# Window attention block: value products ahead of the denominators, sums in a scores' bank, another order of POOL's image bias, values in 64-wide tiles

## What is computed

```
y  = ln(x) rolled by (-4, -4), cut into windows of 64 tokens
q, k, v = y @ qkv_w.T + qkv_b          # q scaled by 16 ** -0.5
p  = softmax(q @ k.T + mask)           # mask: -100 across the seam of the roll
x  = x + unroll(p @ v @ proj_w.T + proj_b)
x  = x + gelu(ln(x) @ mlp_w1.T + mlp_b1) @ mlp_w2.T + mlp_b2
out = x * rsqrt(einsum('nchw,ic->nihw', x * x, gamma) + beta)
```

## Time and profile before

| what | value |
|---|---|
| median of three runs | 1836.98 us |
| the profiled execution | 1833.88 us, span 1832.1 us |
| granted TensorE clock | 0.996 |
| busy: PE, DVE, ACT, POOL | 93%, 81%, 82%, 20% of the span |
| instructions | 83,025 |

### The profile page before, as it was taken

How to read it: one execution, slowest core, us unless ns; L and a number is a source line. 1 busy time by engine, 2 the same in 40 slices (tenths; PEclk the granted TensorE clock), 3 DMA queues, 4 the chain that set the end, 5 groups by cost and what they waited for, 6 DMA issues and landing times.

```text
span 1832.1 us, 83025 instructions
## 1 busy us (share of the span) xinstructions
PE 1712.4 (93%) x33524; PEld 1446.9 (79%) x33524; DVE 1483.5 (81%) x4142; ACT 1501.8 (82%) x2957; POOL 358.5 (20%) x459
## 2 busy tenths in 40 slices
PE   6899999999999999999999999999999999999995
PEld 4788888888888888788888888888888788788784
DVE  5888888888888888888888888888888888888872
ACT  2788888888888888888888888888888888888885
POOL 1112122122121221211221221221221221221211
PEclk9999999999999999999999999999999999999998
DMA  2111221121121121121121122122122122112111
GB/s 55 51 52 54 57 59 54 55 61 55 52 63 54 51 64 55 51 65 53 51 66 53 51 63 56 51 63 56 52 61 57 52 59 59 52 55 63 41 36 33
DMA packets 179168, 100.37 MB, mean 55 GB/s; under 512 B 26868, under 2 KB 178790, under 8 KB 178790
## 3 DMA queue, kind: packets, MB, share of 16 engines
q1 hardware_dynamic: 178228, 94.96, 18.6%
q10 hardware_dynamic: 562, 0.11, 0.0%
HBM read 32.05 MB, written 25.17 MB: 31 GB/s over the span
## 4 chain that ended last, share of the span: by engine, by line
PE 62%; DVE 19%; ACT 11%; issue 6%; DMA 1%; SPq 0%; POOL 0%; DVEq 0%; ACTq 0%; POOLq 0%
PE mm_bank L1107 9%; PE mm_bank L904 8%; PE score_banks L934 6%; PE mm_bank L902 5%; PE mm_bank L1104 5%; PE mm_bank L1092 5%; DVE mean_gap L732 5%; DVE stats L719 5%; PE pv_bank L1057 4%; ACT y_hi L542 4%; ACT y L536 4%; DVE v_block L781 4%; PE turn_banks L940 3%; DVE y_lo L768 3%; PE mm_bank L1071 3%
## 5 line engine op out<-in xcount | busy, mean ns | idle before, releaser
L512 ACT ACT_TABLE_LOAD x256 | 328.4, 1283 | 4.6
L591 ACT ACTIVATE hidden<-mm_bank 128x512 f32<-128x512 f32 x384 | 232.3, 605 | 85.7 <-PE mm_bank L1092 73.7
L1104 PE MATMUL mm_bank<-hidden,w 128*32 128x384 f32 x2304 | 275.0, 490 | 7.0 <-ACT log_sum L577 0.3
L1107 PE MATMUL mm_bank<-hidden,w 128*32 128x128 f32 x2304 | 275.7, 274 | 0.0
L562 ACT ACTIVATE probs<-shifted 128x384 f32<-128x384 f32 x512 | 249.3, 520 | 27.3 <-DVE shifted L797 24.5
L467 POOL TENSOR_TENSOR x<-x,b_bias 128x384 f32<-128x384 f32 x128 | 105.9, 827 | 836.8 <-PE turn_banks L926 836.8
L768 DVE TENSOR_TENSOR y_lo<-turn_banks,y_hi 96x512 fp32r<-96x512 f32 x128 | 87.9, 687 | 194.4 <-ACT y L536 191.4
L1107 PEld LDWEIGHTS mm_bank<-hidden,w 128*32 128x32 f32 x2304 | 242.9, 110 | 0.5
L573 ACT ACTIVATE probs_t<-score_banks 128x512 f32<-128x512 f32 x384 | 219.2, 613 | 0.0
L790 DVE TENSOR_REDUCE row_max<-score_banks 128x6 f32<-128x384 f32 x384 | 209.5, 546 | 0.0
L797 DVE TENSOR_TENSOR shifted<-score_banks,row_max 128x384 f32<-128x384 f32 x384 | 198.8, 544 | 0.0
(11 more groups left out here) (110 smaller groups left out, 4616.1 us busy)
## 6 DMA issues: line engine op xcount, KB each, us to landing
x_ext<-in_x SPq DMA_DIRECT2D x128, 192.0 KB, 3.1
k_block<-k SPq DMA_DIRECT2D x256, 96.0 KB, 2.0
out<-o_ext SPq DMA_DIRECT2D x64, 192.0 KB, 2.4
x_ext<-in_x SPq DMA_DIRECT2D x128, 48.0 KB, 2.8
attended<-attended SPq DMA_DIRECT2D x384, 16.0 KB, 1.8
x<-x SPq DMA_DIRECT2D x384, 16.0 KB, 1.8
out<-o_ext SPq DMA_DIRECT2D x64, 96.0 KB, 2.0
out<-o_ext SPq DMA_DIRECT2D x128, 48.0 KB, 2.2
```

The source lines that it names most:

```text
L512: nc.scalar.preload_act_table_set(name)
L591: nc.scalar.activation(hidden[:, n, :], mm_bank(f"mlp1_{n}", A)[:, :], ACT.Gelu)\
L1104: nc.tensor.matmul(to[group(j), 0:MAIN], w2[:, n, group(j)], hidden[:, n, 128:HALF], start=first, stop=last)
L1107: made = nc.tensor.matmul(to[strip, group(n, 128)], w2[:, c, group(n)], hidden[:, c, 0:128], start=c == 0, stop=c == HID_CHUNKS - 1)
```

## The change

- PE computes `times_v` ahead of `denominators` and `sum_probs`.
- `sum_probs` writes into the first of the scores' banks instead of an `mm_bank`; it then waits for the shift of that bank's scores, and the turns wait for `log_sums`, which reads it. The list of `mm_banks` has one item less.
- PE computes two chunks of `mlp_up` ahead of `turn_in`, not one.
- `project_v` makes 16 products (8 windows, 2 head positions) of 64 tokens by 48 columns instead of 4 of 128 tokens by 96. The values of the second head position come out on partitions 64 to 127. `wv` is laid out for it.
- `v_blocks` is one multiplication of 128x768 elements (the values, each shown twice, times a mask of ones and zeros, `ones_pair_sb`) instead of four copies, so the zeros need not be cleared at the start.
- DVE shifts the first group's scores right behind their maximum.
- ACT's list: the copy of q and the first exponential come ahead of the norm's pair, the denominators' logarithm behind the second exponential, the sums' logarithm behind the third.
- POOL: `bias_x` is the first step of a round, works on the half one round later, and waits for the first maximum of the round.

The core of the diff:

```diff
@@ MM_ITEMS
-            ("sum", ATTEND - 1, log_sum_made, 1, 1),
@@
+        sum_bank = score_banks[:, 0, :]
@@ bias_x
                     wait_alone(pool, x_turned[0], A + 1)
+                    wait_alone(pool, max_ready, SCORE_GROUPS * (A - TURN_IN + 1) + 1)
@@ steps of POOL
+                run(bias_x, TURN_IN - 1)
                 run(wrap_out, DIVIDE)
                 run(wrap_x, TURN_IN + 1)
                 run(bias_x2, PROJECT)
                 run(square, SETTLE)
-                run(bias_x, TURN_IN)
@@ steps of ACT
                 run(k_copy, QK)
+                run(q_copy, QK)
+                run(softmax_exp, ATTEND, GROUPS)
                 rstd_pair(H)
-                run(q_copy, QK)
+                run(softmax_exp, ATTEND, 0)
                 run(log_denominators, DIVIDE)
-                run(softmax_exp, ATTEND, GROUPS)
-                run(softmax_exp, ATTEND, 0)
+                run(softmax_exp, ATTEND, 1)
                 run(log_sums, ATTEND - 1)
-                run(softmax_exp, ATTEND, 1)
                 run(softmax_exp, ATTEND, 2)
@@ v_blocks
-                for n in range(2):
-                    for e in range(TILE_HEADS):
-                        to = v_block[64 * e:64 * e + 64, first + n:first + HALF_WINDOWS:2, :,
-                                     HEAD_DIM * e:HEAD_DIM * (e + 1)]
...
-                        made = nc.vector.tensor_copy(to, values[:, :, :, e, :])
+                nc.vector.tensor_tensor(dst, values.unsqueeze(2).broadcast_to([128, blocks, 2, HEAD_DIM]),
+                                        own_head.unsqueeze(1).broadcast_to([128, blocks, 2, HEAD_DIM]),
+                                        ALU.mult).then_inc(v_ready, 1)
@@ steps of DVE
                 run(max_scores, ATTEND, GROUPS)
+                run(shift_scores, ATTEND, GROUPS)
                 run(max_scores, ATTEND, 0)
-                run(shift_scores, ATTEND, GROUPS)
@@ turn_run
+                    wait(pe, log_sum_made, A)
                     pe.wait_ge(probs_ready, softmax_count(A, 1))
@@ project_v
-                for p in range(PAIRS):
-                    made = nc.tensor.matmul(pv_bank[:, p * DIM:(p + 1) * DIM], y1_windows(A, 2 * p, 2 * p + 2),
-                                            wv[:, :], start=True, stop=True)
+                width = HEAD_PAIRS * HEAD_DIM
+                for n in range(HALF_WINDOWS):
+                    for e in range(TILE_HEADS):
+                        made = nc.tensor.matmul(pv_bank[group(e, 64), n * width:(n + 1) * width],
+                                                y1_windows(A, n, n + 1), wv[:, e, :, :], start=True, stop=True)
@@ times_v
                 pe.wait_ge(v_ready, A + 1)
+                pe.wait_ge(probs_t_ready, GROUPS * (A + 1))
@@ sum_probs
-                pe.wait_ge(probs_t_ready, GROUPS * (A + 1))
-                mm_wait("sum", A)
+                if has(A + 1):
+                    pe.wait_ge(scores_shifted, softmax_count(A + 1, 0))
@@ steps of PE
                 run(project_q, QK)
+                run(times_v, ATTEND - 1)
                 run(denominators, DIVIDE)
                 run(sum_probs, ATTEND - 1)
-                run(times_v, ATTEND - 1)
...
                 run(mlp_up, UP, 0)
+                run(mlp_up, UP, 1)
                 run(turn_in, TURN_IN, 0)
...
                 run(turn_in, PROJECT, 1)
-                run(mlp_up, UP, 1)
                 run(mlp_up, UP, 2)
```

More of the change, by code:

```diff
@@ L97, in window_block @@
         wk = sb("wk", [DIM + 1, DIM])
-        wv = sb("wv", [DIM + 1, DIM])
+        wv = sb("wv", [DIM + 1, TILE_HEADS, HEAD_PAIRS, HEAD_DIM])
         wproj = sb("wproj", [DIM, DIM])
@@ L429, in clear_blocks @@
                     nc.gpsimd.memset(k_block[:, half, :, :], 0.0).then_inc(pads_cleared, 1)
-                nc.gpsimd.memset(v_block[:, :, :, :], 0.0).then_inc(pads_cleared, 1)
             def set_rows():
@@ L576, in log_sums @@
                 act.wait_ge(sums_made, A + 1)
-                nc.scalar.activation(log_sum[:, :], mm_bank("sum", A)[:, 0:MAIN], ACT.Ln)\
+                nc.scalar.activation(log_sum[:, :], sum_bank[:, 0:MAIN], ACT.Ln)\
                     .then_inc(log_sum_made, 1)
@@ L648, in alternating, with heads_first @@
                 return columns.rearrange("c (j d e) -> c j e d", e=TILE_HEADS, d=HEAD_DIM)
+            def heads_first(values):
+                return values.rearrange("c (p e d) -> c e p d", e=TILE_HEADS, d=HEAD_DIM)
             def fold_qkv():
@@ L666, in fold_qkv @@
                     .then_inc(weights_folded, 1)
-                nc.vector.tensor_copy(wv[row, :], qkv_bias[row, 2 * DIM:3 * DIM]).then_inc(weights_folded, 1)
+                nc.vector.tensor_copy(wv[row, :, :, :], heads_first(qkv_bias[row, 2 * DIM:3 * DIM])).then_inc(weights_folded, 1)
                 dve.wait_ge(column_sums, 1)
-                for n, folded in enumerate((wq[0:DIM, :], wk[0:DIM, :], wv[0:DIM, :])):
+                for n, folded in enumerate((wq[0:DIM, :], wk[0:DIM, :], wv[0:DIM, :, :, :].rearrange("c e p d -> c (e p d)"))):
                     nc.vector.scalar_tensor_tensor(folded, score_banks[0:DIM, 1, n * DIM:(n + 1) * DIM],
@@ L771, in v_blocks @@
                 dve.wait_ge(v_made, A + 1)
-                if A == 0:
-                    dve.wait_ge(pads_cleared, 3)
-                first = (A % 2) * HALF_WINDOWS
-                for n in range(2):
-                    for e in range(TILE_HEADS):
-                        to = v_block[64 * e:64 * e + 64, first + n:first + HALF_WINDOWS:2, :,
-                                     HEAD_DIM * e:HEAD_DIM * (e + 1)]
-                        values = pv_bank[64 * n:64 * n + 64, 0:PAIRS * DIM]\
-                            .rearrange("k (p m e d) -> k p m e d", m=HEAD_PAIRS, e=TILE_HEADS, d=HEAD_DIM)
-                        made = nc.vector.tensor_copy(to, values[:, :, :, e, :])
-                made.then_inc(v_ready, 1)
+                blocks, first = HALF_WINDOWS * HEAD_PAIRS, (A % 2) * HALF_WINDOWS
+                dst = v_block[:, first:first + HALF_WINDOWS, :, :].rearrange("k n p (e d) -> k (n p) e d", e=2)
+                values = pv_bank[:, 0:blocks * HEAD_DIM].rearrange("k (i d) -> k i d", d=HEAD_DIM)
+                own_head = ones_pair_sb[:, :].rearrange("k (e d) -> k e d", e=2)
+                nc.vector.tensor_tensor(dst, values.unsqueeze(2).broadcast_to([128, blocks, 2, HEAD_DIM]),
+                                        own_head.unsqueeze(1).broadcast_to([128, blocks, 2, HEAD_DIM]),
+                                        ALU.mult).then_inc(v_ready, 1)
             def group_scores(g):
@@ L1063, in sum_probs @@
             def sum_probs(A):
-                pe.wait_ge(probs_t_ready, GROUPS * (A + 1))
-                mm_wait("sum", A)
+                if has(A + 1):
+                    pe.wait_ge(scores_shifted, softmax_count(A + 1, 0))
                 for m in range(HEAD_PAIRS):
-                    nc.tensor.matmul(mm_bank("sum", A)[group(m), 0:MAIN], ones_pair_sb[:, :],
+                    nc.tensor.matmul(sum_bank[group(m), 0:MAIN], ones_pair_sb[:, :],
                                      probs_t[:, A % 2, m, 0:LAST, :], start=True, stop=True)
                 for m in range(HEAD_PAIRS):
-                    made = nc.tensor.matmul(mm_bank("sum", A)[strip, group(m, 128)], ones_pair_sb[:, :],
+                    made = nc.tensor.matmul(sum_bank[strip, group(m, 128)], ones_pair_sb[:, :],
                                             probs_t[:, A % 2, m, LAST, :], start=True, stop=True)
```

2 lines of the change are left out of this document (1 added, 1 removed).

## The result

| | before | after |
|---|---|---|
| median of 4 runs each on one chip | 1837.06 us (1836.83 to 1837.54) | 1776.66 us (1774.62 to 1777.75) |
| ratio | | 0.967, interval 0.9657 to 0.9683 |
| span of the profiled execution | 1832.1 us | 1776.0 us |
| granted TensorE clock | 0.996 | 0.989 |
| round, median of the two kinds, from first maximum to first maximum | 12.91 and 14.68 us | 13.26 and 13.27 us |

What follows compares the result with a forecast made beforehand. Mostly PE work bounds the kernel, with `bias_x` holding `mean_gap` every second round. Rounds fall from 13.815 to 13.33 us; 0.485 over 120 rounds, 58 us, off 1833.88 gives 1775.7, plus 3.1 gives 1779 us, range 1743 to 1828.

Steps and rivals of the forecast that it cites:

- The hold: DVE's `mean_gap` stands still during POOL work on SBUF: 1.58 us in every second round becomes 0.8 in every round.
- rival 1: At the round's end the square does not hold `mean_gap`: rounds average 12.84 us, total 1720 us; chance 0.20.
- Values in 64-wide tiles: `project_v` on PE: 16 products on two tiles side by side take 0.92 us, bounds 0.67 and 1.84.
- rival 2: In the values on PE, weight loads queue up: 1.84 us, round 14.25, total 1889 us; chance 0.06.
- where the form changes: On PE behind the values, the tiling change was counted at 0; at 0.29 us it would be 35 us.
- The sums' wait for the second shift: On PE, the sums wait for the shift of the scores' bank they write: 0.02 us, start at 2.70.
- the two chunks: On PE, two way-up chunks ahead of the turns in take 1.57 us.
- ACT: Denominators' logarithm behind two exponentials: done near 3.65, wanted by the way down at 4.05, hidden with 0.4 us to spare.
- The saved 0.48 is worth nothing here: On DVE, one values operation saves 0.48 us over four copies, gaining nothing because the statistics wait for the turn in.
- The chunk costs more than the wait gave: On PE, the second way-up chunk removes the wait for `y_lo`, but the turns in stood ready 0.34 us earlier before.
- Image bias: `bias_x` on POOL beside DVE instructions reading PSUM costs nothing; upper bound 0.24 us in every second round.
- The ends: Filling and draining the pipeline, outside the some 120 full rounds, were counted at nothing.

Runs made afterwards that it cites:

- e4: Changed kernel with `bias_x` back at its old place, last on POOL: 1905.68 us, ratio 1.0368 to the kernel before.
- e6: Kernel before the change with only `bias_x` moved, to first on POOL behind the first maximum: 1800.22 us, ratio 0.9792.
- e7: Changed kernel with `bias_x2` moved to the next round, behind `bias_x` and the first maximum, on POOL: 1735.71 us, ratio 0.9436.
- e2: Changed kernel with the values as before, 4 products and four copies: 1757.38 us, ratio 0.9565.
- e3: Changed kernel with one way-up chunk ahead of the turns in, as before: 1760.78 us, ratio 0.958.
- e8: e7 with the values as before, 4 products and four copies: 1742.25 us, ratio 0.9477.
- e9: e7 with one way-up chunk ahead of the turns in: 1756.10 us, ratio 0.9552.

## Why the prediction was right, step by step

The walk through one round against the round from 912.43 to 925.69 (times from the first maximum):

| step | forecast | measured |
|---|---|---|
| first shift | 0.60 | 0.58 |
| value products | 1.30 | 1.28 |
| denominators | 1.97 | 1.95 |
| sums | 2.70 | 2.60 |
| turns | 6.15 | 6.03 |
| values | 7.55 | 7.43 |
| first way up | 8.47 | 8.50 |
| turns in, of x and of x2 | 10.04, 10.39 | 10.00, 10.33 |
| `bias_x2`, square | 11.07, 11.86 | 11.01, 11.79 |
| end of the square | 12.90 | 12.82 |
| `mean_gap` ready, ended | 12.08, 12.93 | 12.05, 12.86 |
| next maximum | 13.33 | 13.26 |

- **The hold.** The mechanism was right: the long hold of every second round went, one of 0.8 us came into each, and the next maximum starts 0.40 after `mean_gap`. e4, e6 and e7 show it from three sides. Of rival 1 the price was right too, as e7 shows; it didn't happen, because the square does not come clear of `mean_gap` by itself.
- **Values in 64-wide tiles.** This term was mis-sized: taken 0.92, measured 1.07 (920.93 - 919.86), between the bounds and below the 1.41 from which rival 2 decides. The passes themselves came out close to the 0.90 that the rate of the value products gave: the last of them starts 0.92 after the first (920.78 - 919.86). Most of what was missing is in the step behind them, where the form changes, which the prediction counted at 0. The last value product by itself, after and then before:

```profile
920.78 0.22 PE L1007 MATMUL pv_bank<-wv,y 97*64 97x48 f32 x1
923.13 0.28 PE L1004 MATMUL pv_bank<-wv,y 97*128 97x96 f32 x1
```

  The first way-up product starts 0.15 behind it after (920.93), and 0.06 before (923.19), where the form doesn't change; in e2, the changed kernel with the old values, it is 0.06 too. That the change of form is the reason was not tested apart from the values themselves. The rule of the Trainium skill, "TensorE: Matmul & The Clock Gate", Part 3, under which the loads would have queued (1.84), does not hold in this trace.
- **The sums' wait for the second shift** was counted at 0.02, with 2.70 as the start. They start at 2.60, right behind the denominators, which take 0.65 and not 0.71, so there was no wait. This 0.10 and 0.07 less for the two chunks (1.50, not 1.57) set off the 0.15 of the values, and that is luck: by estimate the round would have been 0.17 longer without these two, 20 us in 120 rounds, still within the stated range.
- **ACT.** `log_den` was to be hidden with 0.4 us to spare; it ends at 915.89, 3.46 into the round, and the way down starts at 3.90.
- **"The saved 0.48 is worth nothing here", "The chunk costs more than the wait gave":** both right, by e2 and e3, and both only as long as the square sets the round, as e8 and e9 show.
- **Image bias.** Free, as counted: over the whole trace the shifts in the scores' banks take a median of 0.546 us beside `bias_x` (63 of them) and 0.546 elsewhere (321).
- **The ends.** Filling and draining were counted at nothing. From the first to the last of the maxima the trace lost 61.9 us (1739.2 to 1677.3), and the two ends grew by 5.7 (29.4 to 30.7 ahead, 63.5 to 67.9 behind): 56.1 in the span. The forecast's 58 is near it by luck in part: the 120 rounds that it counted, for the 127 between the maxima, set off the ends that it counted at nothing.

## What to carry to other kernels

Look at which engine ends the round before pricing an edit: the same two edits lost 19 and 16 us while POOL's square set the round, and gained 6.5 and 20 once it didn't. When two engines keep each other out of a memory, move the longer work beside instructions that are not affected, and ask of work that is to come earlier when its own input lands. A walk of one round with every duration from a row of the trace told this round within 0.07 us. A term that was new to the trace was off by 0.15, and two others happened to set it off.

## What the runs show of the hardware

- **A waiting DVE instruction is not let in between two POOL operations.** In e4 `mean_gap` waits from 904.28, the square ends at 905.06 and `bias_x`, begun at 905.02, runs its full 1.50 us first; `mean_gap` ends at 906.55. So the hold here is the rest of the square and all of `bias_x`. e4's forecast counted on it; the kernel before shows it too, with 1.58 us.
- **Two tiles of 64 columns side by side gave no gain on PE.** The same values cost 0.91 us as 8 passes of 128 loaded columns and 1.07 us as 32 passes of 64 on two tiles, in fp32; 0.09 of the 0.16 is the longer step to the next product (0.15 instead of 0.06).
- **A PE idle time of 2.12 us was followed by some 6 us with a mean granted clock of 0.72** (e4). The hold's price is then not only the wait. Not every such idle time was followed by one: in e4 the stretch from 963 to 966 has PE busy for 0.87 us of 3, and the one behind it has a clock of 1.00. Of the 57 idle times of this kind in e4 (1.9 us or more ahead of the value products), 25 were followed by a fall of the clock. What decides it stays open.
